# A rule for choosing ScalarE's activation tables, and new orders of the steps on all engines

## The reference

```
mamba(u): z0, x0, xBC, dt = split(u @ W_in.T)          # 512, 512, 544 and 8 columns are used
          dt = softplus(dt + bias);  A = -exp(A_log)
          xBC = silu(causal conv of 4 taps over the 1024 positions(xBC) + b)
          x, B, C = split(xBC)                         # 8 heads of 64; 16 states
          h_t = exp(dt A) h + dt x B;  y_t = h C + D x  # a scan over 1024 positions
          y = layernorm(y);  y = sigmoid(y @ W_gate.T + b) * y
          return concat(silu(z0) * x0, y) @ W_out.T
ffn(x):   h = gelu(x @ ternary(W_fc));  h = layernorm(h);  return h @ ternary(W_proj)
```

## Time and profile before

| | us |
|---|---|
| median of 3 runs | 1126.93 |
| profiled execution | 1132.95 |
| its span | 1131.2 |
| PE busy | 1073.9 |
| PEld busy | 681.4 |
| DVE busy | 986.0 |
| ACT busy | 949.3 |
| POOL busy | 461.7 |
| ACT's table loads, 117 | 150.1 |

### The profile page before, as it was taken

One profiled execution on the slowest core, in us unless ns is written; L12 is line 12 of the kernel. 1 busy time (PEld: TensorE's weight loads), 2 busy tenths in 40 slices (PEclk: granted clock), 3 DMA queues, 4 the chain that ended last, 5 costly groups with the idle time before them and its releaser, 6 DMA issues. The chain is left out here.

```text
span 1131.2 us, 23010 instructions
## 1 busy us (share of the span) xinstructions
PE 1073.9 (95%) x8214; PEld 681.4 (60%) x8214; DVE 986.0 (87%) x1967; ACT 949.3 (84%) x1678; POOL 461.7 (41%) x568
## 2 busy tenths in 40 slices
PE   3899999999999999999999999999999999999996
PEld 1464756556565756657565565656666565746664
DVE  5999999998889989989989988898998799777666
ACT  5877589889879889998989869898988987878785
POOL 1223344434433545244543524443552443445542
PEclk9978999999999999999999999999999999989999
DMA  6612332345435344564536253454457255423758
GB/s 193 187 39 47 96 59 61 75 77 125 76 77 104 87 92 95 104 103 83 106 83 111 51 114 75 97 79 102 89 98 131 47 96 85 85 50 63 141 103 159
DMA packets 306706, 105.92 MB, mean 94 GB/s; under 512 B 275488, under 2 KB 302880, under 8 KB 306592
## 3 DMA queue, kind: packets, MB, share of 16 engines
q1 hardware_dynamic: 306592, 104.46, 46.7%
HBM read 24.32 MB, written 8.39 MB: 29 GB/s over the span
## 5 line engine op out<-in xcount | busy, mean ns | idle before, releaser
L392 PE MATMUL bank<-xnT,win 128*128 128x512 f16 (+1 forms) x1248 | 300.1, 388 | 21.5 <-DMA xnT<-hb 17.5
L392 PEld LDWEIGHTS bank<-xnT,win 128*128 128x128 f16 (+1 forms) x1248 | 122.5, 102 | 158.0 <-DVE win L915 17.4
L1022 DVE SCALAR_TENSOR_TENSOR cv<-bank,cws,cv 128x510 f32<-128x510 f32 (+5 forms) x240 | 177.5, 744 | 14.6 <-ACT tail L722 5.4
L392 PE MATMUL bank<-yhl,wg 128*128 128x512 f16 x768 | 174.4, 382 | 6.0 <-DVE cv L1022 3.9
L182 ACT ACT_TABLE_LOAD x117 | 150.1, 1283 | 2.8 <-PEq L1491 0.7
L392 PEld LDWEIGHTS bank<-yhl,wg 128*128 128x128 f16 x768 | 74.3, 98 | 96.8 <-DVE cv L1022 4.9
L625 PE MATMUL bank<-wpj,hT 128*128 128x256 f16 x1024 | 121.2, 273 | 7.8 <-DMA hT<-hb 6.3
L1298 POOL TENSOR_TENSOR caty<-tg,caty 128x512 f16<-128x512 f32 x64 | 80.4, 1268 | 113.2 <-ACT caty L824 113.2
L1302 POOL TENSOR_TENSOR cat<-sz,cat 128x512 f16<-128x512 f32 x64 | 81.6, 1280 | 108.3 <-ACT cat L836 108.2
L1293 POOL TENSOR_TENSOR yT<-yhl 128x512 f32<-128x512 f16 x64 | 77.6, 1235 | 117.7 <-DMA yhl<-ynh 117.7
L613 PE MATMUL bank<-wfc,x3T 128*128 128x512 f16 x512 | 122.4, 379 | 0.9 <-DMA x3T<-hb 0.5
(11 more groups left out here) (148 smaller groups left out, 2062.5 us busy)
## 6 DMA issues: line engine op xcount, KB each, us to landing
x<-in_x SPq DMA_DIRECT2D x31, 512.0 KB, 4.1
out_y<-x SPq DMA_DIRECT2D x15, 512.0 KB, 3.0
crep<-cv SPq DMA_DIRECT2D x128, 32.0 KB, 2.0
hT<-hb SPq DMA_TRANSPOSE x128, 3.3
caty<-in_wg SPq DMA_DIRECT2D x1, 1024.0 KB, 7.1
x<-in_wout SPq DMA_DIRECT2D x1, 1024.0 KB, 7.1
hT<-in_wfc SPq DMA_DIRECT2D x1, 1024.0 KB, 10.7
hb<-in_wpj SPq DMA_DIRECT2D x1, 1024.0 KB, 7.7
```

What stands on the lines that cost most here:

```text
L392: m = eng.matmul(b, lhs(p, k), rhs(q, k), start=(n == 0), stop=(n == len(seq) - 1))
L1022: op = eng.scalar_tensor_tensor(cs[0:w, j, 3 - k:T], b[0:w, 0:T - 3 + k], cws[0:w, j, k:k + 1], cs[0:w, j, 3 - k:T], ALU.mult, ALU.add)
```

## The change

Each function now has a tuple of sets that serve it: Exp the set of exp and the set with exp and ln, Tanh the sets of Silu, Gelu and exp. At the start ACT's queue gets the list of functions that its steps will need (`todo`), and each `load` takes the first off it. If the table at hand does not serve the step, `load` takes, among the sets that do, the one that serves the longest run of steps to come. The exp of softplus (`dt_first`) asks for Ln's set, which holds exp too, as a ln follows it.

All five orders are replaced. They hold the same steps, in the same number, in other places: 917 on PE, 1115 on ACT, 1114 on DVE, 419 on POOL, 334 on SP. Bank numbers in `PE_ORDER` change too. Apart from these and the table loads no instruction changes.

```diff
-SETS = {"Exp": "natural_log_exp_and_others", "Ln": "natural_log_exp_and_others", "Gelu": "gelu_and_others",
-        "Silu": "silu_and_others"}
+SETS = {"Exp": ("exp_and_others", "natural_log_exp_and_others"), "Ln": ("natural_log_exp_and_others",),
+        "Gelu": ("gelu_and_others",), "Silu": ("silu_and_others",),
+        "Tanh": ("silu_and_others", "gelu_and_others", "exp_and_others")}
+
+NEEDS = {"N": "Exp", "1": "Ln", "3": "Ln", "e": "Exp", "f": "Exp", "E": "Exp", "b": "Silu", "s": "Silu", "z": "Silu",
+         "t": "Tanh", "g": "Gelu"}
 
 PE_ORDER = (
...
-    "e03 q006 O07 q043 q057 z00 c16 r04320 w0 w0 q015 c27 c26 m11 w0 w0 z15 y04 y03 B02 s10 b15 y00 x12 x14 x13 "
-    "u21 e12 g14 y03 x11 q127 q127 c25 v12 t17 c21 C00 c23 z17 G06 G05 G01 G03 r16540 g27 m22 q113 w1 w1 q121 z13 "
...
+    "t05 q071 O00 q067 q021 c15 c24 r03067 w0 w0 q021 v05 w0 w0 s12 m11 z15 y03 y00 y02 y06 B07 c25 u23 x11 x10 "
+    "e13 c22 c23 x16 q171 z17 g11 c20 q144 b14 G05 x12 v14 t16 G02 G05 C03 q102 G06 r17415 m23 g26 w1 w1 q130 v12 "
...
-    "vf4 vf0 zf6 zf2 pd5 Gf3 Gf7 fe1 fe6 pd4 Gf3 Gf2 pd7 pd1 fe6 fe5 fe0 fe3 fe2 fe6 of4 of7 of5 of1 pe0 ff3 ff2 "
-    "ff6 pe4 ff7 ff5 ff1 pe0 ff3 pe2 ff6 pf7 pf5 pf1 pf3 "
...
+    "oe1 oe6 vf2 Gf0 vf3 Gf4 pd1 vf6 fe2 fe0 fe5 fe4 fe3 pd7 Gf6 Gf2 pd0 pd5 fe4 fe6 fe2 of1 of7 of0 of5 ff3 ff4 "
+    "pe6 ff2 pe1 ff7 ff0 ff5 pe3 ff4 pe6 ff2 pf7 pf0 pf1 pf5 "
 )
 ACT_ORDER = (
-    "N0 a0 h0 a0 h0 W0 W0 c0 c0 a1 h1 10 c0 30 c0 z0 b0 z0 c0 c1 40 c1 l0 50 s0 z0 c1 s0 f0 l0 F0 c1 a2 F0 l0 e0 "
...
+    "a0 h0 W0 a0 h0 W0 N0 c0 c0 a1 h1 c0 c0 10 30 z0 b0 c0 z0 s0 40 c1 s0 c1 l0 50 a2 h2 z0 c1 l0 F0 11 c1 f0 F0 "
...
@@ class Queue
         self.table = None
+        self.todo = []
...
-    def holds(self, func):
-        if func == "Tanh":
-            return self.table in ("gelu_and_others", "silu_and_others")
-        return func not in SETS or self.table == SETS[func]
-
     def load(self, func):
-        if not self.holds(func):
-            self.table = SETS.get(func, "silu_and_others")
+
+        if self.table not in SETS[func]:
+            self.table = max(SETS[func], key=lambda t: next((n for n, f in enumerate(self.todo) if t not in SETS[f]), 9999))
             self.eng.preload_act_table_set(self.table)
+        self.todo = self.todo[1:]
...
             act = Queue(eng)
+            act.todo = [NEEDS[letter] for letter, _, _, _ in steps_of(ACT_ORDER) if letter in NEEDS]
...
             def dt_first(i, n):
-                act.load("Exp")
+                act.load("Ln")
                 act.wait_ge(dt_min, i + 1)

```

## The result

The changed kernel takes 1138.14 us (median of 5 runs, 1131.94 to 1139.35) against 1126.42 us for the kernel before beside it. The ratio over all executions is 1.0086 (95% interval 1.0069 to 1.0102; the two medians alone divide to 1.0104): slower by about 0.9%. The median lies above the range of the prediction, which ended at 1131.2 us. A second series of the same kernel gave 1137.76 us, ratio 1.0106 [1.0089, 1.0123].

A forecast was written before the change was run, and what follows sets the result against it. PE, busy 1073.9 of 1131.2 us, was taken as the bound, with DVE pacing the pipeline's filling. Terms 0 + 0.2 + 0 - 1.0 - 2.3 + 1.0 - 1.4 = -3.5 us gave 1123.4 us unprofiled, range 1116.4 to 1131.2.

The forecast's parts named there:

- Loads: ACT's table loads: 117 before and after at 1283 ns, ACT busy 949 us again; term 0.
- the crossed cases: Table loads by walking ACT's orders: 114 for the old order with the new rule, 126 for the new order with the old.
- Start: Kernel start: weight copies ahead of the second half of x delay it; +0.2 us, bounds 0 and +1.3.
- Filling the pipeline: 20 to 130 us, paced by DVE: largest lateness DVE causes PE is 32.1 before, 32.2 after; term 0.
- The clock: Low clock from 72 us: denser large products should bring it back sooner; -1.0 us, bounds 0 and 13.2.
- 130 to 1040: Long stretch, PE 97.9% busy: bank reuse -2.3 us and a shorter cover of yT +1.0 us.
- bank reuse: 130 to 1040 us: banks retaken within 4 us fall from 228 to 201, PE's idle time shrinks 12%; -2.3 us.
- cover of yT: Behind a block's last w: PE work covering DVE's yT falls from 68.0 to 43.3 us over blocks 5 to 14; +1.0 us.
- The slower rival: Wait for yT takes over: 7.9 us uncovered against 1.9, +6.0 us; up to 1131.2 us; chance 0.26.
- The end: Last block: the 1.4 us wait before the first output product goes; -1.4 us, bounds -1.4 and +3.

The follow-up runs named there:

- e5: The changed kernel itself, unchanged, timed and profiled a second time; 1137.76 us, ratio 1.0106 to the kernel before.
- e3: Against the changed kernel: new rule and new orders up to the last w of block 1, the old orders behind; ratio 1.0070 to the kernel before.
- e4: Against the changed kernel: new rule, old orders up to the last w of block 1, the new orders behind; ratio 1.0009 to the kernel before.
- e6: Against the changed kernel: PE's first gate product of block 0 moved behind block 1's last x transpose and t step; 1135.51 us, ratio 1.0087.
- e17: Against the changed kernel: on DVE, the tap of block 2's fourth conv chunk moved ahead of block 1's b step; 1136.96 us, ratio 1.0078.
- e18: Against the changed kernel: e17's edit, plus PE's second x step of block 1 ahead of its first G step and a later u step; 1135.96 us, ratio 1.0083.
- e1: Against the kernel before: the new rule for table loads with all five old orders; ratio 1.0016.

## Why the prediction was wrong

**Loads: right.** 117 of 1283 ns, and 114 and 126 for the crossed cases. ACT's busy time, 945.7 us, is 3.3 below the forecast 949, for which 2 us were allowed. The Trainium skill ("ScalarE: Activation LUTs", What ACT_TABLE_LOAD costs) has a drain of about 1380 ns beside the load; ACT idles 2.1 us before 117 loads in after, so this trace too shows none.

**Start: within its own spread.** +0.2 was forecast. In after PE's first product came at 17.07 us instead of 17.46; but GpSimd's result, and with it ACT's first x step, came at 8.54 us and not at 9.05. In e5, the same program, the x step came at 9.04 and PE's first product at 17.58, 0.1 later than before.

**Filling the pipeline: this step failed.** It read "the largest is 32.1 before and 32.2 after: 0". The term was put at nothing. The sum was right as a sum: DVE's work up to block 1's yT is 96.3 us before and 96.7 after. But it counted only by how much DVE makes PE late. It took for granted that DVE, which paces the stretch, never stands still, in the new order as in the old. DVE stood still 3.9 us before and 7.8 to 12.7 after, most of the difference for b and x steps that PE's order has behind q, c and gate steps. In place of 0 the term measured 4.4 us at yT1 in after's profiled execution and 9.4 in e5's. e3 and e4 show that the opening's orders carry the loss, and the traces that DVE waits there; which waits cost the median is open, since e6, e17 and e18 took some of them out and their ratios stayed within the spread of the changed kernel. The prediction's own test for this step was too loose: it asked for a DVE share under 90% from 20 to 130 us, and the share was 93% (102.2 of 110; 96% before). The question "which of PE's small steps does the pacing engine need next, and what now stands ahead of them?" was never put. The answer was in the order: block 1's b moved 14 PE steps back and its last x 7, behind the large products that the next term counted as a gain.

**The clock: right from 72 to 96 us, wrong behind it.** With the denser products the granted clock between 72 and 96 us was 0.73 in after and 0.77 in e5, 0.57 before; -1.0 us was forecast for it. But the next 12 us, at 1.00 before, had 0.97 in after and 0.50 in e5, and there DVE waits for PE's small steps. Over the stretch to yT1 the clock of e5 was 0.86, no better than before. With that same mean DVE idled 3.9 us in the old order and 12.7 in the new, so a lower mean clock alone isn't the cause. Products that hold a bank until DVE or ACT read it are not a gain to an engine that then waits for these.

**130 to 1040: no effect where -1.3 was forecast** (bank reuse -2.3, cover of yT +1.0). PE's idle time stayed at 19.4 and 19.6 us, and e4 shows the new rest as level. The count of short bank reuses, 228 to 201, said nothing of waiting here. The wait of the y transposes for DVE's yT is 2.7 us where it was 1.9, which is the +1.0. The slower rival had 7.9 there; it fell, and the loss came from elsewhere; the measured median lies beyond that rival's 1131.2 us too.

**The end: right.** The wait before the first output product went. Block 15's, in after (compare, which has 1.37 us of idle time):

```profile
1087.41 2.75 PE L615 MATMUL bank<-wfc,x3T 128*128 128x512 f16 x12
1090.00 1.47 PE L394 MATMUL bank<-wout,cat 128*128 128x256 f16 x12
```

PE's idle time behind 1040 us fell by 2.0, though the waits for transposed h rose from 6.3 to 8.0 us.

**What stays open.** Why the granted clock is lower in some executions of the same program isn't settled. Over nine executions of the changed kernel the time goes with the mean clock: 1131.9 and 1134.0 us for the two at 0.986 and 0.985, and 1136.7 to 1140.0 for the seven at 0.980 to 0.983. Over 63 executions of the kernel before, beside the experiments and on four chips, the mean is 1127.7 us at 0.988 (22 of them) and 1129.4 at 0.986 (15). Between 84 and 112 us PE in e5 has five waits of 0.7 to 2.0 us for ACT and DVE. The Trainium skill ("TensorE: Matmul & The Clock Gate", A second HAM failure mode: psum-queue depth-cycling) says that small idle times between groups of matmuls, where banks are cycled, are enough to make the clock swing between its levels. The traces agree as far as both are there together; after has four of the same five waits, and a clock of 0.97 between 96 and 108 us, so no run shows the one as the cause of the other. Nor is it shown which single engine's order loses the opening. One engine's old opening beside the others' new ones wasn't tried.

## What to carry to other kernels

In a statically ordered kernel find the engine that paces the stretch and list what it waits for in both directions. Here its idle time in the filling of the pipeline came back one to one at the end, with a nearly full stretch behind it. Before a large product is moved ahead of a small transpose, ask who reads the small one next and who must empty the banks that the large one fills. This finds the wait, and not yet the cure: moving single steps here mostly gave another wait for the first. And profile the same program more than once before stages are compared.

## What the runs showed of the hardware

Two profiled executions of one program were 5.0 us apart at 125 us: from 96 to 108 us one had a granted clock of 0.97 and the other 0.50. First after, then e5, with the columns of the earlier trace rows:

```profile
96.00:108.00 12.00, 10.62 (x81) 5.81 (x82) 8.98 (x13) 7.31 (x11) 6.63 (x10) 0.97 0.17 32
```

```profile
96.00:108.00 12.00, 10.62 (x31) 4.65 (x32) 5.44 (x8) 5.33 (x8) 5.08 (x7) 0.50 0.16 30
```

PE is busy 10.62 us in both and does 81 matmuls in one and 31 in the other. The counts exaggerate the difference, as after's hold the 32 small ones of a t step that e5 does only at 110.7 us; the same gate step took 2.76 and 5.30 us. A busy share without the clock beside it hides this.

The executions of one kernel spread over several us: 7.4 us over 5 of after and 3.3 over 4 of e5, 10.4 over 12 of e1, and for the kernel before 1.1 over 5, 4.3 over 7 and 4.6 over 23. All 117 table loads of after, those of the exp set among them, take 1283 ns.
